# GNN kernel: backward counts of groups with a forward matrix kept as bytes, VectorE adds byte and bf16 chunks, one PSUM bank per kind of count

## What is computed

```
def _L1_gnn_ref(x, edge_index, W, bias, num_nodes):     # both directions
    src = concatenate([src0, dst0, loop]); dst = concatenate([dst0, src0, loop])
    deg = segment_sum(ones, dst);  dis = rsqrt(max(deg, 1))
    agg = segment_sum(x[src] * (dis[src] * dis[dst])[:, None], dst)
    return relu(agg @ W.T + bias)
# L2: row -> col with self loops, counts, prelu;  L3: three convolutions with edge weights
x = layernorm(x + L0(x)); x = layernorm(x + L1(x)); x = layernorm(x + L2(x)); x = layernorm(x + L3(x))
```

## Time and profile before

| | us |
|---|---|
| median of 3 runs | 4412.11 (4409.29 to 4418.47) |
| the profiled execution | 4412.28 |
| its span in the trace | 4410.5 |
| TensorE busy | 3810.4 (86%) |
| VectorE busy | 2944.6 (67%) |
| ScalarE busy | 1529.5 (35%) |
| count stage, wide rows (430 to 1600 us) | 1170 |
| layer 1 (1763 to 2331 us) | 568 |

### The profile page before, as it was taken

One profiled execution on the slowest core, in us unless ns is written; L12 is line 12 of the kernel. 1 busy time (PEld: TensorE's weight loads), 2 busy tenths in 40 slices (PEclk: granted clock), 3 DMA queues, 4 the chain that ended last, 5 costly groups with the idle time before them and its releaser, 6 DMA issues. The chain is left out here.

```text
span 4410.5 us, 83016 instructions
## 1 busy us (share of the span) xinstructions
PE 3810.4 (86%) x30818; PEld 2546.0 (58%) x30818; DVE 2944.6 (67%) x6093; ACT 1529.5 (35%) x3170; POOL 2815.0 (64%) x2363
## 2 busy tenths in 40 slices
PE   5887999998988865688987986999899999998998
PEld 4766888887878754344444443455445555554444
DVE  8899999999999868355553344466356666523665
ACT  3334566665656546000000000333134444412332
POOL 3876888888888810566635774777266666606773
PEclk7778999998999977899998998999999999998999
DMA  4444777777777753999976775999655555537997
GB/s 140 133 126 133 231 247 240 238 237 225 248 236 238 228 201 115 290 322 322 323 260 211 240 233 167 329 323 327 219 204 195 185 199 191 193 109 278 331 318 263
DMA packets 612904, 1019.51 MB, mean 231 GB/s; under 512 B 90888, under 2 KB 417575, under 8 KB 612111
## 3 DMA queue, kind: packets, MB, share of 16 engines
q1 hardware_dynamic: 476700, 773.91, 51.5%
q0 software_dynamic: 90848, 199.74, 15.3%
q10 hardware_dynamic: 44956, 40.55, 2.8%
HBM read 737.12 MB, written 276.78 MB: 230 GB/s over the span
## 5 line engine op out<-in xcount | busy, mean ns | idle before, releaser
L925 POOL DMA_INDIRECT x<-p_table,src_i x832 | 1218.5, 1464 | 344.5 <-issue 241.8
L1514 POOL DMA_INDIRECT rows_b<-x_table,low_src x552 | 574.9, 1041 | 485.1 <-POOLq L144 206.4
L1514 POOL DMA_INDIRECT rows_a<-h_table,low_src x412 | 448.1, 1088 | 240.1 <-DVE split_l3b L1805 120.4
L904 ACT CAST st_cnt<-ps_mat 128x512 bf16<-128x512 f32 (+1 forms) x825 | 440.9, 590 | 444.5 <-PE ps_deg L819 384.3
L1593 PE MATMUL po_l3b<-mat_l3b,rows_b 128*128 128x512 f32 (+1 forms) x1372 | 570.9, 564 | 19.6 <-DMA mat_l3b<-weights_fwd 18.6
L1593 PE MATMUL po_l3a<-mat_l3a,rows_a 128*128 128x512 f32 (+1 forms) x882 | 375.0, 572 | 30.0 <-DMA mat_l3a<-weights_fwd 29.3
L1593 PE MATMUL po_l3c<-mat_l3c,rows_a 128*128 128x512 f32 (+1 forms) x882 | 375.3, 573 | 13.9 <-DMA mat_l3c<-weights_fwd 13.2
L1593 PE MATMUL po_l<-mat_l,rows_a 128*128 128x512 bf16 (+1 forms) x1323 | 296.2, 380 | 99.8 <-DVE mat_l L1833 99.0
L1593 PEld LDWEIGHTS po_l3b<-mat_l3b,rows_b 128*128 128x128 f32 x1372 | 241.6, 195 | 241.5 <-issue 221.1
L834 PE MATMUL ps_mat<-rows_a,hot_s 128*128 128x128 bf16 x4851 | 360.8, 226 | 9.0
L677 DVE TENSOR_TENSOR rows_a<-rows_a,slots 128x1792 bf16<-128x1792 bf16 (+1 forms) x198 | 366.8, 1886 | 1.4
(11 more groups left out here) (415 smaller groups left out, 7448.8 us busy)
## 6 DMA issues: line engine op xcount, KB each, us to landing
weights_fwd<-st_wt SPq DMA_DIRECT2D x396, 256.0 KB
mat_l<-counts_fwd SPq DMA_DIRECT2D x112, 896.0 KB
mat_l3a<-weights_fwd SPq DMA_DIRECT2D x56, 1792.0 KB
mat_l3c<-weights_fwd SPq DMA_DIRECT2D x56, 1792.0 KB
counts_rev<-st_cnt SPq DMA_DIRECT2D x588, 128.0 KB
rev_l<-counts_rev SPq DMA_DIRECT2D x84, 896.0 KB
mat_l3b<-weights_fwd SPq DMA_DIRECT2D x42, 1792.0 KB
counts_fwd<-st_cnt SPq DMA_DIRECT2D x396, 128.0 KB
```

What stands on the lines that cost most here:

```text
L904: nc.scalar.copy(st_cnt[:, q, :, j * 2 * P:j * 2 * P + n_col], ps_mat[:, f % 3, :].rearrange("p (d c) -> p d c", d=2)[:, :, 0:n_col]).then ...
L925: pool.indirect_dma_start(ring[:, j % RING, t * FD:(t + 1) * FD], None, p_table, bass.IndirectOffsetOnAxis(src_i[:, j * TH + t:j * TH + t ...
L1514: pool.indirect_dma_start(ring[:, j % RL, t, :], None, table, bass.IndirectOffsetOnAxis(low_src[:, j * TH + t:j * TH + t + 1].bitcast(U32), 0)
```

## The change

- The backward counts lie in DRAM in the order in which layer 1 reads them: `counts_rev[g, :, u, :]` for the four low groups in bf16, and `bytes_rev[g - 4, :, u, :]` in unsigned bytes for groups 4 to 12. A partition's seven blocks of a chunk are one unbroken piece, 7168 bytes or 3584 bytes, where they were seven pieces of 1024.
- In layer 1 the chunk of backward counts of a forward group is loaded as bytes into half of its old buffer (`rev8`), and VectorE adds bf16 and bytes. Low groups load and use bf16 as before.
- In the count stage each kind of count has a bank of its own: forward counts of the sub, backward counts of the sub, weights. TensorE's matmuls of a sub are ordered by that. ScalarE copies 512 unbroken columns to `st_fwd`, `st_rev` (bf16, or bytes for subs 4 to 12) and `st_wt`. The last sub of a row, with one block, fills three banks where it filled two.

```diff
         counts_fwd = nc.dram_tensor("counts_fwd", [NB, P, NP], BF16).ap()
-        counts_rev = nc.dram_tensor("counts_rev", [NB, P, NP], BF16).ap()
+        REV_LOW = LOWS[0] // GB
+        counts_rev = nc.dram_tensor("counts_rev", [REV_LOW, P, NB, GB * P], BF16).ap()
+        bytes_rev = nc.dram_tensor("bytes_rev", [GROUPS - REV_LOW, P, NB, GB * P], U8).ap()
         weights_fwd = nc.dram_tensor("weights_fwd", [NB, P, NP], F32).ap()
...
             hot = sb("hot", [P, 4, TH, W], F32, c)
-            st_cnt = sb("st_cnt", [P, STAGES, 2, 4 * P], BF16, c)
+            st_fwd = sb("st_fwd", [P, STAGES, 4 * P], BF16, c)
+            st_rev = sb("st_rev", [P, STAGES, 4 * P], BF16, c)
+            st_rev8 = st_rev[:].rearrange("p q e -> p (q e)").bitcast(U8).rearrange("p (q e) -> p q e", q=STAGES)
             st_wt = sb("st_wt", [P, STAGES, 4 * P], F32, c)
...
 
-                return min(u, NARROW) * SUBS + max(u - NARROW, 0) * (NK + SUBS)
+                return min(u, NARROW) * SUBS + max(u - NARROW, 0) * 3 * SUBS
 
             def fill_of(u, s, part):
 
-                return fills_before(u) + (s if u < NARROW else 3 * s + min(part, len(sub_pairs(s))))
+                return fills_before(u) + (s if u < NARROW else 3 * s + part)
 
...
                             pe.wait_ge(slots_ready, 2 * u + 2)
-                        for j, k in enumerate(sub_pairs(s)):
-                            f = fill_of(u, s, j)
+                        pairs = [(j, k, [q for q in range(2) if 2 * k + q < NB]) for j, k in enumerate(sub_pairs(s))]
+
+                        def bank(part):
+
+                            f = fill_of(u, s, part)
                             if f >= 3:
                                 pe.wait_ge(evicted, f - 2)
-                            b = f % 3
-
-                            rev_at = 2 * P * j if u < NARROW else 2 * P
+                            return ps_mat[:, f % 3, :]
+
+                        def outward(j, k, q):
+
+                            return nc.tensor.matmul(ps_deg[:, 2 * k + q:2 * k + q + 1], hot_s[:, h, j0 + j, q * P:(q + 1) * P],
+                                                    slots[:, u % 2, NV, k:k + 1], start=False, stop=False)
+
+                        if u >= NARROW:
+                            to = bank(0)
+                            for j, k, halves in pairs:
+                                for q in halves:
+                                    nc.tensor.matmul(to[:, (2 * j + q) * P:(2 * j + q + 1) * P],
+                                                     hot_s[:, h, j0 + j, q * P:(q + 1) * P], hot_d[:, h, j0 + j, :],
+                                                     start=True, stop=True)
+                                    mm = outward(j, k, q)
+                            mm.then_inc(filled, 1)
+                        to = bank(1)
+                        for j, k, halves in pairs:
+                            if u < NARROW:
+                                for q in halves:
+                                    outward(j, k, q)
                             rows = hot_d[:, h, j0 + j, :]
-                            halves = [q for q in range(2) if 2 * k + q < NB]
-                            for q in halves:
-                                half = hot_s[:, h, j0 + j, q * P:(q + 1) * P]
-                                if u >= NARROW:
-                                    nc.tensor.matmul(ps_mat[:, b, q * P:(q + 1) * P], half, rows, start=True, stop=True)
-                                nc.tensor.matmul(ps_deg[:, 2 * k + q:2 * k + q + 1], half, slots[:, u % 2, NV, k:k + 1],
-                                                 start=False, stop=False)
-                            nc.tensor.matmul(ps_mat[:, b, rev_at:rev_at + len(halves) * P], rows,
+                            nc.tensor.matmul(to[:, 2 * P * j:(2 * j + len(halves)) * P], rows,
                                              hot_s[:, h, j0 + j, 0:len(halves) * P], start=True, stop=True)
                             mm = nc.tensor.matmul(ps_deg[:, 64 + 4 * u:68 + 4 * u], rows, slots[:, u % 2, 2:NV + 1, k],
                                                   start=False, stop=False)
-                            if u >= NARROW:
-                                mm.then_inc(filled, 1)
+                        mm.then_inc(filled, 1)
                         if u < NARROW:
-                            mm.then_inc(filled, 1)
                             return
-                        f = fill_of(u, s, 2)
-                        if f >= 3:
-                            pe.wait_ge(evicted, f - 2)
-                        for j, k in enumerate(sub_pairs(s)):
-                            for q in range(2):
-                                if 2 * k + q < NB:
-                                    half = hot_s[:, h, j0 + j, q * P:(q + 1) * P]
-                                    for v in range(3):
-                                        mm = nc.tensor.matmul(ps_mat[:, f % 3, (2 * j + q) * P:(2 * j + q + 1) * P], half,
-                                                              hot_w[:, h, v, j0 + j, :], start=(v == 0), stop=(v == 2))
+                        to = bank(2)
+                        for j, k, halves in pairs:
+                            for q in halves:
+                                for v in range(3):
+                                    mm = nc.tensor.matmul(to[:, (2 * j + q) * P:(2 * j + q + 1) * P],
+                                                          hot_s[:, h, j0 + j, q * P:(q + 1) * P],
+                                                          hot_w[:, h, v, j0 + j, :], start=(v == 0), stop=(v == 2))
                         mm.then_inc(filled, 1)
...
                             act.wait_ge(staged_out[q], 16 * sum(stores(i) for i in range(q, n, STAGES)))
-                        for j, k in enumerate(sub_pairs(s)):
-                            f = fill_of(u, s, j)
-                            if u < NARROW:
-                                break
+                        for part, stage in enumerate((st_fwd, st_rev if s < REV_LOW else st_rev8, st_wt)):
+                            if u < NARROW and part != 1:
+                                continue
+                            f = fill_of(u, s, part)
                             act.wait_ge(filled, f + 1)
-                            n_col = min(2 * P, NP - k * 2 * P)
-                            nc.scalar.copy(st_cnt[:, q, :, j * 2 * P:j * 2 * P + n_col], ps_mat[:, f % 3, :].rearrange(
-                                "p (d c) -> p d c", d=2)[:, :, 0:n_col]).then_inc(evicted, 1)
-                        f = fill_of(u, s, 2)
-                        act.wait_ge(filled, f + 1)
-                        to = st_cnt[:, q, 1, 0:w] if u < NARROW else st_wt[:, q, 0:w]
-                        nc.scalar.copy(to, ps_mat[:, f % 3, 0:w]).then_inc(evicted, 1)
+                            nc.scalar.copy(stage[:, q, 0:w], ps_mat[:, f % 3, 0:w]).then_inc(evicted, 1)
                         if place(u, s) is not None:
...
                         sp.wait_ge(evicted, fill_of(u, s, 2) + 1)
-                        sp.dma_start(counts_rev[u, :, cols], st_cnt[:, q, 1, 0:sub_cols(s)]).then_inc(staged_out[q], 16)
+                        if s < REV_LOW:
+                            sp.dma_start(counts_rev[s, :, u, :], st_rev[:, q]).then_inc(staged_out[q], 16)
+                        else:
+                            sp.dma_start(bytes_rev[s - REV_LOW, :, u, 0:sub_cols(s)], st_rev8[:, q, 0:sub_cols(s)]
+                                         ).then_inc(staged_out[q], 16)
                         if u >= NARROW:
-                            sp.dma_start(counts_fwd[u, :, cols], st_cnt[:, q, 0, 0:sub_cols(s)]).then_inc(staged_out[q], 16)
+                            sp.dma_start(counts_fwd[u, :, cols], st_fwd[:, q, 0:sub_cols(s)]).then_inc(staged_out[q], 16)
                             sp.dma_start(weights_fwd[u, :, cols], st_wt[:, q, 0:sub_cols(s)]).then_inc(staged_out[q], 16)
...
 
-            both = len(mats) == 2
+            both = len(mats) == 3
             exact = kind not in ("relu", "prelu")
...
                 rev = sb(f"rev_{name}", [P, REVS, CHK, GB * P], BF16, c) if both else None
+                rev8 = rev[:].rearrange("p q s m -> p (q s m)").bitcast(U8).rearrange(
+                    "p (q h s m) -> p q h s m", q=REVS, h=2, s=CHK)[:, :, 0] if both else None
                 once = 1 if exact else 2
...
                                             sp.wait_ge(chunk_used, n - REVS + 1)
-                                    sp.dma_start(rev[:, n % REVS, :, 0:nb * P],
-                                                 mats[1][ch * CHK:(ch + 1) * CHK, :, g * GB * P:(g * GB + nb) * P].rearrange(
-                                                     "s p m -> p s m")).then_inc(rev_in[n % REVS], 16)
+                                    to, given = (rev8, mats[2][g - REV_LOW]) if has_fwd[p] else (rev, mats[1][g])
```

(6 more changed lines are left out.)

1 line of the change is left out of this document (added).

## The result

The changed kernel is slower. Its median is 4437.9 us (12 runs, 4423.2 to 4454.9), that of the kernel before on the same chip 4414.2 us (12 runs, 4402.0 to 4422.1): a ratio of 1.0053, 95% interval 1.0038 to 1.0069. The forecast was 4378 us, and 4437.9 lies outside its range. A single execution far above the others at a lower granted clock, as one of e16's twelve (5503.6 us, 0.64 in place of 0.92), is left out of a ratio.

What follows compares the result with a forecast made beforehand. Bandwidth was taken to bound layer 1's forward groups, with VectorE the bound after the change; group gains of 7.7, 10.3, 5.2, 6 and 5 us, count stage nothing, made 34 us off 4412.3: 4378 us. The range takes in 4343 and 4416.

Steps and rivals of the forecast that it cites:

- What bounds layer 1 before: Layer 1: bandwidth bounds the eight forward groups, some 8 to 11 us each above TensorE's pace of 35.6 us.
- The load: Layer 1, gain: backward chunk halved to 0.459 MB, 9.2 us less a group of seven; bandwidth alone would give 65 us.
- The add: Layer 1, cost: VectorE's add of 3584 elements goes from 2.03 to 3.88 us, at one element a cycle.
- Rivals A: Layer 1: the add keeps 2.03 us and transfers bound the groups; 70 us gained, 4342 us; chance 0.12.
- C: Rival, layer 1: slower add; gain used up at 4.9 us, kernel 4433 us at 5.6 us; chance 0.10.
- VectorE's work: Layer 1: a forward group's steps, finishes and seven adds of 3.82 us keep VectorE busy 41.4 us.
- the walk: Layer 1, step-by-step run of chunks: a single forward group ends at 38.8 us, a pair at 83.7 us.
- the sum: Layer 1: gains of forward groups 4 to 11 added up, together 34 us of 4412.3 us.
- The count stage at nothing: Count stage: new matmul order, copies and byte output cost nothing, as VectorE sets the stage; ±4 us.
- So VectorE becomes the bound of the forward groups: Layer 1: VectorE's 41.4 us exceeds TensorE's 35.6 and transfers' 36.5, by 5.8 us a group; the traffic's 65 us don't all arrive.
- What the profile should have shown: Signs: add 3.9 us, VectorE's wait for the backward chunk under 60 us, pairs 84, low groups 35.6, count stage 1170 ± 4.
- TensorE still waiting for the add: Sign that the forecast is right: in layer 1 TensorE still waits for the add, mostly in chunks 6 and 7 of a run.

Runs made afterwards that it cites:

- e16: Changed kernel with each byte add as four instructions of 896 elements: 4405.1 us, ratio 0.9994 to the kernel before.
- e13: Changed kernel, but ScalarE widens most byte chunks to bf16 before the add, and each backward load is requested one chunk earlier: 4363.2 us, ratio 0.9900 to before.
- e14: e2 (all counts bf16) with each backward load requested one chunk earlier: 4398.3 us, ratio 0.9980 to the kernel before.
- e8: Changed kernel with the add over only 512 of a chunk's 3584 elements, the other backward counts left out of the result: ratio 0.9919 to before.
- e2: Changed kernel with its banks and reading-order layout, but backward counts all in bf16, no bytes: 4402.5 us, ratio 0.9966 to the kernel before.
- e4: Changed kernel without layer 1's gathers behind the first four steps, whose rows are used again: 4386.2 us, ratio 0.9935 to the kernel before.
- e1: Kernel before with only the change's banks and order of TensorE's matmuls in the count stage: 4412.2 us, ratio 0.9990.
- e12: Kernel before with each add as two instructions over every second element, no bytes or new layout: ratio 1.0161.
- e3: Kernel before with its bf16 add run through the elements in another, strided order: 5111.7 us, ratio 1.157.

## Why the prediction was wrong, point by point

- **What bounds layer 1 before**: right. With half the backward bytes and short adds (e13) the forward groups came down to 41 us, and with all of them (e14) not. The 36.5 us that bandwidth alone would allow were not reached: with the add nearly gone (e8) the seven groups took 39.3 us in the mean.
- **The load**: right in direction, the DMA share fell from 0.91 to 0.73. That unbroken pieces by themselves bring 13 us (e2) was no term of mine.
- **The add**: 3.88 us forecast, 3.894 measured. The bound from L634 and L677 held to 0.4%. Rivals A (2.03 us) and C (4.9 us and more) didn't come about; that C's price, 4433 us, is near the result is chance.
- **VectorE's work**: 41.4 us a group forecast, 40.7 and 39.2 in the windows of the pairs, and 85 us for a pair without gathers (e4) where the walk had 83.7. Layer 1 of e4 is 28 us shorter than before; the sum had 34.
- **The count stage at nothing**: right, as far as the scatter of its end (1760 to 1780 us in the changed kernel) lets one see: 0.9990 for the banks in e1, VectorE busy 1079.1 of 1170 us (1082.0 before), and byte output costs a cast nothing (before 599 ns):

```profile
L917 ACT CAST st_rev<-ps_mat 128x512 uint8<-128x512 f32 x392 | 231.9, 598 | 178.3 <-PE ps_deg L838 164.4 <-DMA bytes_rev<-st_rev 5.9 <-DMA counts_rev<-st_rev 5.3
```

- **The step that failed**: "So VectorE becomes the bound of the forward groups". I compared three paces, TensorE 35.6, transfers 36.5, VectorE 41.4, and left out the fourth: GpSimd's gathers, which feed the same steps. Their pace, 35 us a group, followed from the windows that I used for the others, 57 us busy in a pair, and 0.3 more between two gathers. And a gather that comes up beneath an add does not run beside it; it stops. What the runs showed in place of VectorE's 41.4 us: 50.1 us a forward group, set by the gathers, and 43.0 once these were taken out (e4). Both were to be seen in the trace of before, at an add that ended at 1836.73 us: start, us.

```profile
1833.54 0.94 POOL L1514 DMA_INDIRECT rows_b<-x_table,low_src  x1 [0.30 <-issue]
1834.78 2.77 POOL L1514 DMA_INDIRECT rows_b<-x_table,low_src  x1 [0.30 <-issue]
```

  The same instruction on the same bytes, 2.77 us beside 0.94. Had I asked why, 7 x 1.9 us of longer add would have gone on GpSimd's path too: 35 + 13 = 48 us, above the 45.8 of a forward group before, and the forecast would have been slower. That is still 2 us short of the 50.1.
- **What the profile should have shown**: low groups at 35.6 and the add at 3.9 came. VectorE's wait for the backward chunk fell from 181 to 93 us, not under 60, and pairs took 101 us in place of 84. "TensorE still waiting for the add" had company: 47.9 us for rows.

## What to carry over

When one instruction gets longer, list every engine that shares a step with it and give each its own pace, the gathers of GpSimd included; then look in the trace for the same instruction with two durations and find out what ran beside the long one. A long two-input VectorE instruction can cost more than its own time, and cutting it in four won here although the sum of the pieces was longer; look at the gathers in the trace whether they really get in between, since beneath the halves of e12 they mostly did not. And when a stage is put between a load and its use, move the request for that load forward by as much.

## What the runs showed of the hardware

- An indirect gather that started beneath a VectorE add of two SBUF operands ended 0.82 us after the add, for adds of 3.9 us and of 2.0 (in e13, add 2002.85 to 2004.88, gather 2003.70 to 2005.70). Beside nothing it took 0.95 us, and so did one that was running when an add began. With four pieces of 1.09 us a gather was held by one piece, with two strided halves of 2.25 us mostly by both.
- A bf16 add over 3584 elements took 2.03 us in plain order, 4.5 us as two halves with a step of 4 bytes, and 16.1 us with steps of 256 bytes and 1 KB (e3), 4.5 ns an element.
- A bf16 plus byte add took 3.89 us for 3584 elements; ScalarE's widening of as many 3.18 us.
- Pairs of forward groups moved 359 GB/s with backward counts in pieces of 7 KB and 348 with pieces of 1 KB, at a lower DMA share (0.98 to 1.05); the forward counts had pieces of 1792 bytes in both.
